# Attention stage of an audio tower: another spacing of the value products, and minima by reductions

## The reference, cut to what matters

```python
hd = C // H; g = hd // 3            # 8 heads of 24 channels, three parts of 8
q3, q4, q5 = (q[..., :g], q[..., g:2 * g], q[..., 2 * g:])   # likewise k and v
x3 = merge(_attn(q4, concat([k3, k4]), concat([v3, v4]), scale))
x4 = merge(_attn(q5, concat([k3, k5]), concat([v3, v5]), scale))
x5 = merge(_attn(q5, concat([k4, k5]), concat([v4, v5]), scale))
out = concat([x3, x4, x5], axis=2);  return out @ w_proj.T + b_proj
```

## Time and profile before

| | |
|---|---|
| median of 3 runs | 1832.63 us (1830.71 to 1834.19) |
| profiled execution | 1832.84 us, span 1831.1 us |
| DVE instructions of attention, first to last block | about 399 to 1381 us of the span |
| busy over the span | PE 95%, DVE 82%, ACT 79%, POOL 68% |
| granted TensorE clock, mean | 0.981 of full speed |

### The profile page before, as it was taken

One profiled execution on the slowest core, in us unless ns is written; L12 is line 12 of the kernel. 1 busy time (PEld: TensorE's weight loads), 2 busy tenths in 40 slices (PEclk: granted clock), 3 DMA queues, 4 the chain that ended last, 5 costly groups with the idle time before them and its releaser, 6 DMA issues. The chain is left out here.

```text
span 1831.1 us, 56113 instructions
## 1 busy us (share of the span) xinstructions
PE 1736.6 (95%) x19008; PEld 1020.6 (56%) x19008; DVE 1497.6 (82%) x3546; ACT 1438.5 (79%) x2983; POOL 1253.9 (68%) x2306
## 2 busy tenths in 40 slices
PE   5999999599999999999999999999984999999999
PEld 3677777244444444444444444444443777777776
DVE  6877777689999999999999999999965555565554
ACT  4667676289999999999999999999974777777775
POOL 5677776467777777777777777777734656565651
PEclk9999999699999999999999999999997999999999
DMA  7344442144444444444444444444431333333232
GB/s 196 93 114 115 115 115 69 28 83 93 92 92 94 93 91 95 92 93 92 92 94 93 90 95 92 93 92 91 94 56 34 73 69 70 70 68 71 65 74 52
DMA packets 503935, 159.49 MB, mean 87 GB/s; under 512 B 452176, under 2 KB 503120, under 8 KB 503888
## 3 DMA queue, kind: packets, MB, share of 16 engines
q1 hardware_dynamic: 503888, 158.90, 41.0%
HBM read 37.26 MB, written 12.48 MB: 27 GB/s over the span
## 5 line engine op out<-in xcount | busy, mean ns | idle before, releaser
L753 DVE TENSOR_REDUCE tops<-p_maxa 128x6 f32<-128x762 f32 x512 | 483.6, 945 | 23.2 <-PE p_maxa L583 22.4
L660 PE MATMUL p_o<-probs,vn 127*32 127x256 f32 x6144 | 411.0, 385 | 0.4 <-DVE att L780 0.4
L703 ACT ACTIVATE probs<-p_s 128x512 f32<-128x512 f32 x512 | 305.3, 596 | 86.1 <-PE p_s L579 85.7
L757 DVE TENSOR_REDUCE tops<-p_maxb 128x4 f32<-128x508 f32 x512 | 346.3, 676 | 0.0
L579 PE MATMUL p_s<-qm,kt 32*128 32x256 f16 x3072 | 341.0, 273 | 3.0 <-DMA qm<-qk 0.7
L710 ACT ACTIVATE probs<-p_s 128x512 f32<-128x512 f32 x512 | 310.7, 607 | 2.3 <-PE p_s L579 2.2
L707 ACT ACTIVATE probs<-p_s 128x512 f32<-128x512 f32 x512 | 304.7, 595 | 0.0
L1062 DVE TENSOR_TENSOR gel_lo<-gel,gel_hi 128x512 f16<-128x512 f32 x192 | 151.7, 790 | 168.6 <-ACT gel_hi L1034 168.5
L579 PEld LDWEIGHTS p_s<-qm,kt 32*128 32x128 f16 x3072 | 135.8, 92 | 223.7 <-issue 127.0
L660 PEld LDWEIGHTS p_o<-probs,vn 127*32 127x32 f32 x6144 | 160.7, 109 | 141.0 <-issue 74.7
L808 POOL TENSOR_TENSOR qk<-raw,one 128x384 f16<-128x384 f32 x128 | 105.9, 827 | 185.4 <-ACT raw L728 185.4
(11 more groups left out here) (212 smaller groups left out, 4529.0 us busy)
## 6 DMA issues: line engine op xcount, KB each, us to landing
xt_a<-in_xt SPq DMA_DIRECT2D x32, 512.0 KB, 4.4
xt_b<-in_xt SPq DMA_DIRECT2D x64, 256.0 KB, 5.2
out<-out_sb SPq DMA_DIRECT2D x32, 336.0 KB, 2.6
xt<-hx SPq DMA_TRANSPOSE x128, 2.4
kt<-qk SPq DMA_TRANSPOSE x128, 2.8
qt<-qk SPq DMA_TRANSPOSE x128, 2.4
qm<-qk SPq DMA_TRANSPOSE x128, 2.7
yt<-ay SPq DMA_TRANSPOSE x128, 2.3
```

The source lines that it names most:

```text
L660: last = nc.tensor.matmul(p_o[32 * j:32 * j + 32, blocks, :], vn[0:NP, r, src:src + 32], probs[0:NP, r % 2, QUAD * g + j, kind * 256:(kind ...
L703: nc.scalar.activation(probs[:, r % 2, h + 1, 0:512], p_s[1][:, :, :].rearrange("p x n -> p (x n)"), ACT.Exp, scale=SCALE).then_inc(act_e1 ...
L753: nc.vector.tensor_reduce(top[:, q, 6 * pair:6 * pair + 6].rearrange("p (e k) -> p e k", e=2), p_ma[:, :, :].rearrange("p (e k) n -> p e k ...
L757: nc.vector.tensor_reduce(top[:, q, 24 + 4 * fourth:28 + 4 * fourth], p_mb[:, :, 0:NP], AX.X, ALU.max, negate=True)\
```

## The change

In PE's order of `attend`, `outputs(., 0, 1)` moves from behind unit 3 of its block to behind unit 0 of the next body, and `outputs(., 1, 0)` from behind unit 0 to behind unit 1. Calls behind units 3, 0, 1 are then one, two, three instead of two, two, two. The minima become three reductions instead of two operations on two tensors; so that each reduces neighbouring elements, the key parts are stored in the order 3, 5, 4 (the weights' columns are permuted on the host, and the names `K3, K5, K4` index them; the `p_maxb` products then read blocks 0 and 2 instead of 0 and 1).

```diff
                 products(i, r, 0)
+                outputs(i - 1, before, 0, 1)
                 outputs(i - 1, before, 0, 2)
+
+                products(i, r, 1)
                 outputs(i - 1, before, 1, 0)
-
-                products(i, r, 1)
                 outputs(i - 1, before, 1, 1)
                 outputs(i - 1, before, 1, 2)
...
                 products(i, r, 3)
                 proj(i)
                 outputs(i, r, 0, 0)
-                outputs(i, r, 0, 1)
...
-                    nc.vector.tensor_tensor(low[:, 0].rearrange("p (g j) -> p g j", g=2), of4[:, 0], of4[:, 1], ALU.min)
-                    nc.vector.tensor_tensor(low[:, 1:3], of5[:, 0:2], of5[:, 2:3].broadcast_to([128, 2, HEADS]), ALU.min).then_inc(dve_min, 1)
+                    nc.vector.tensor_reduce(low[:, 0].rearrange("p (g j) -> p g j", g=2),
+                                            got[:, 24:40].rearrange("p (j g k) -> p g j k", g=2, k=2), AX.X, ALU.min)
+                    of5 = got[:, 0:24].rearrange("p (h k) -> p h k", k=3)
+                    for pair in range(2):
+                        last = nc.vector.tensor_reduce(low[:, 1 + pair], of5[:, :, pair:pair + 2], AX.X, ALU.min)
+                    last.then_inc(dve_min, 1)
...
-                    maximum(p_mb[:, 0:2, :], fourth, 0, slice(0, 2), 0)
-                    maximum(p_mb[:, 2:4, :], fourth, 0, slice(0, 2), 1).then_inc(pe_mb[u], 1)
+                    maximum(p_mb[:, 0:2, :], fourth, 0, slice(K3, K4 + 1, 2), 0)
+                    maximum(p_mb[:, 2:4, :], fourth, 0, slice(K3, K4 + 1, 2), 1).then_inc(pe_mb[u], 1)
```

More of the change, by code:

```diff
@@ L459, in attend @@
         K0 = NQ * 32
+        K3, K5, K4 = range(3)
         scaled, moved = sb("scaled", [128, C]), sb("moved", [128, 1])
@@ L598, in odd @@
                     if do:
-                        score(p_s[1][:, 2:4, :], b, 1, slice(0, 3, 2)).then_inc(pe_s1[u], 1)
+                        score(p_s[1][:, 2:4, :], b, K4, slice(0, 3, 2)).then_inc(pe_s1[u], 1)
                         pe.wait_ge(act_e5[u - 1] if u else act_e5[3], seen(i + 1 if u else i))
-                        score(p_s5[:, 0:2, :], fifth, 2, slice(1, 3), 0)
-                        score(p_s5[:, 2:4, :], fifth, 2, slice(1, 3), 1).then_inc(pe_half[u], 1)
+                        score(p_s5[:, 0:2, :], fifth, K5, slice(1, 3), 0)
+                        score(p_s5[:, 2:4, :], fifth, K5, slice(1, 3), 1).then_inc(pe_half[u], 1)
                 if has_s:
@@ L607, in products @@
                     pe.wait_ge(act_e1[u - 1] if u else act_e1[3], seen(i + 1 if u else i))
-                    score(p_s[1][:, 0:2, :], b, 0, slice(0, 2))
+                    score(p_s[1][:, 0:2, :], b, K3, slice(0, 2))
                 if u == 2:
@@ L616, in products @@
                     pe.wait_ge(act_e0[u - 1] if u else act_e0[3], seen(i + 1 if u else i))
-                    score(p_s[0][:, 0:2, :], a, 0, slice(0, 2))
-                    score(p_s[0][:, 2:4, :], a, 1, slice(0, 3, 2)).then_inc(pe_s0[u], 1)
+                    score(p_s[0][:, 0:2, :], a, K3, slice(0, 2))
+                    score(p_s[0][:, 2:4, :], a, K4, slice(0, 3, 2)).then_inc(pe_s0[u], 1)
                 if has_m:
                     pe.wait_ge(dve_mb[u - 1], seen(i + 2 if u < 3 else i + 3))
-                    maximum(p_mb[:, 0:2, :], fourth, 0, slice(0, 2), 0)
-                    maximum(p_mb[:, 2:4, :], fourth, 0, slice(0, 2), 1).then_inc(pe_mb[u], 1)
+                    maximum(p_mb[:, 0:2, :], fourth, 0, slice(K3, K4 + 1, 2), 0)
+                    maximum(p_mb[:, 2:4, :], fourth, 0, slice(K3, K4 + 1, 2), 1).then_inc(pe_mb[u], 1)
             def rows(o, x, name, bias=None):
@@ L766, in body @@
                     got = top[:, (r + 1) % 2]
-                    of5 = got[:, 0:24].rearrange("p (h k) -> p k h", k=3)
-                    of4 = got[:, 24:40].rearrange("p (j g k) -> p k g j", g=2, k=2)
                     low = slots((r + 1) % 2, 0, NQ)[:, :, 24].rearrange("p (x h) -> p x h", x=3)
-                    nc.vector.tensor_tensor(low[:, 0].rearrange("p (g j) -> p g j", g=2), of4[:, 0], of4[:, 1], ALU.min)
-                    nc.vector.tensor_tensor(low[:, 1:3], of5[:, 0:2], of5[:, 2:3].broadcast_to([128, 2, HEADS]), ALU.min).then_inc(dve_min, 1)
+                    nc.vector.tensor_reduce(low[:, 0].rearrange("p (g j) -> p g j", g=2),
[4 more added lines that the diff above has]
+                    last.then_inc(dve_min, 1)
                 maxima(i, r, 2)
@@ L1193 @@
     v = w[:, 2 * C:].reshape(C, 3, GRP, QUAD, G8).transpose(0, 1, 3, 2, 4).reshape(C, C)
-    arr["wqkv"] = np.concatenate([w[:, C // 3:2 * C], v], axis=1)
+    k3, k4, k5 = (w[:, C + x * C // 3:C + (x + 1) * C // 3] for x in range(3))
+    arr["wqkv"] = np.concatenate([w[:, C // 3:C], k3, k5, k4, v], axis=1)
     arr["wproj"] = np.asarray(L0_attn_w_proj).T.reshape(3, GRP, QUAD, G8, C).transpose(0, 2, 1, 3, 4).reshape(C, C)
```

## The result

The changed kernel takes 1868.45 us (1866.27 to 1870.03, four runs) against 1831.97 of the kernel before beside it: ratio 1.0192, 95% interval 1.0177 to 1.0208. It is slower, by 36 us and not by the 51 of the forecast; that lies at the lower edge of the stated range, just outside it when the ratio is applied to the earlier median (1.0192 x 1832.63 = 1867.8).

A forecast was written before the change was run, and what follows sets the result against it. The prediction took a loop of PE and DVE through unit 2's read as the bound: 0.41 us longer in each of 125 blocks, 51 in all, so 1832.84 + 51 = 1884 us, range 1868 to 1896.

The forecast's parts named there:

- the stated range: Whole kernel: 1868 to 1896 us, meant to hold 8 of 10, around the forecast of 1884.
- What bounds the kernel, and the place of the cost: Loop of PE and DVE through units 0, 1, 2; a third call behind unit 1 makes the block 0.41 us longer.
- first stretch: DVE, from the end of unit 0's p_maxb read to unit 2's p_maxa read: 2.02 us grows to 2.43.
- a second holder of the same place: PE's unit 1: ACT's third exponential, ending at 807.89, also holds it; its getting out of the way buys only 0.02.
- Does the second stretch give it back? ... So no: DVE, unit 2's read to the end of unit 0's next p_maxb read: stays 5.78 us, its idle place unchanged.
- 125 x 0.41 = 51: Sum over attention's 125 steady blocks: each 0.41 us longer, so 51 us more in all.
- Minima: DVE between units 1 and 2: three reductions take 0.3 us instead of 0.52; covered, so they cost or give nothing.
- the 0.4 named: Sign of being right: DVE idle about 0.4 us before line 753 once a block, put down to PE's p_maxa.
- The third: Rival: PE starts unit 1's p_maxb products earlier in some blocks, or DVE's second stretch shrinks; 1858 us, chance 6%.
- The first and second: Rivals: PE's lead holds through units 0 and 1, 1833 us, 3%; DVE's minima set unit 2, 1805 us, 3%.
- The fourth: Rival: ACT's lateness behind the p_o copy adds 0.1 a block, 1897 us, or PE's clock falls, 1891; chance 8%.
- ACT: Copy of p_o starts 0.41 us later; the 0.63 wait at the next unit 0 covers it, with 0.2 left.

The follow-up runs named there:

- e4: Kernel before without POOL's operation that makes the keys' low halves, so that kt and qt are issued earlier: 1825.66 us (0.9955).
- e9: Changed kernel plus one POOL operation (128x192) ahead of the signal that releases the kt and qt DMAs: 1881.11 us (1.0275).
- e3: Changed kernel plus one POOL operation (128x64) ahead of the signal that releases the kt and qt DMAs: 1868.9 us (1.0196).
- e1: Kernel before with only the value products moved as in the changed kernel, minima left as two operations on two tensors: 1867.89 us (1.0189).
- e7: Changed kernel with unit 2's p_maxa products issued before its scores, as in the other units: 1866.55 us (1.0189).

## Why the prediction came out as it did

- *What bounds the kernel, and the place of the cost: right for the changed kernel.* PE's lead won behind unit 3 ended at unit 1's `p_maxb` products, where PE now waits for DVE's read in every block, and the loop through unit 2's read grew from 2.02 to 2.44 in its first stretch, as worked out (2.43). Three calls there take 1.44 (811.73 to 813.17), where two took 1.00. In the kernel before, the profile puts PE's wait in unit 1 down to ACT's third exponential instead (line 710, 29.8 us in 103 blocks), which the forecast had as a second holder of the same place; so the loop named was one of several of nearly the same length, as e4 shows. From the table of waits after:

```profile
PEld p_maxb L584 <- DVE tops L758: 19.3, 99, 0.3
```

- *"Does the second stretch give it back? ... So no": this step failed.* The forecast took the idle time before line 777 as fixed, since the transposes "move with" unit 2's products. They do not keep their distance: in the kernel before, the distance held a wait of PE for the `qt` DMA inside unit 2. With the unit 0.41 later the keys had landed, the unit got 0.13 shorter on average, and DVE's reciprocal stood 1.49 instead of 1.61 behind its read. The term 125 x 0.41 = 51 should have been 125 x (0.41 - 0.13) = 35; measured 36. e9 brings the wait back and pays for it; e4 takes it away in the kernel before, and the wait before the reciprocal goes with it.
- *How it was missed.* The text had the number: `qt` lands at 809.37, "before today's `p_maxa` products of unit 2", so no change. (The trace has 809.41 for this block.) But the unit's scores had started at 809.33, and what should have been compared with the landing was that time, at which the product could have started. That its start followed the landing at the same 0.10 in every block, and not the scores, was the sign of a wait. A steady distance from the issue alone does not show one: before it is 2.52 to 2.56, but the changed kernel keeps 2.68 to 2.71 as closely and does not wait: in e3 the distance is 2.57 and the time is the same. The wait before DVE's read gave no hint, because line 753 hangs on the other of the two products. And the idle time of 0.07 was too small a price for it: the reciprocal also lost the 0.06 by which it could start before the read ahead ends.
- *Minima: right.* Three reductions took 0.33 (812.85 to 813.18; the forecast had 0.3) and changed no time. The idle time before the read is 0.61 rather than the 0.4 named, since it also holds the 0.2 by which the minima got shorter. e1 has the same idle time with two-tensor minima, which no longer started beside line 831.
- *The rivals.* The third, half given back by a shrinking second stretch (1858), named the place but not a mechanism; a third was given back. The first and second did not happen. The fourth had PE's busy share fall to 93.7% and the clock with it; the share is 783.04 of 800, or 97.9%, and the clock stayed at 1.00.
- *ACT.* Its wait before the copy of `p_o` appeared as expected (46.3 us in 99 blocks), and its wait at unit 0 shrank (0.27 in one block, 0.63 before); the time shows no trace of either.

## What to carry to other kernels

A landing ahead of an instruction's start does not mean that nothing waited: compare the landing with the time at which the instruction could have started. Look over many blocks. Here the start kept one distance from the landing (0.10) while its distance from the work ahead varied (0.11 to 0.19), and that was a wait; in a steady loop a constant distance by itself is none. When a change moves work later, list the waits that it lets run out as well as those that it lengthens; part of the price comes back there. Where two engines hold each other at several places of one loop, loosening one place alone can move the idle time to the next, as in e7 and e4.

## What was not expected of the hardware

Products of one unit can start out of their written order, so that "strictly in the written order" above does not hold for the starts on PE. After the change the `p_maxb` product that starts at 813.36 is written behind both `p_maxa` products and starts ahead of the second of them (813.41); so it is in each of 99 blocks, and in none of the 103 before. One `p_maxa` product runs at once with the scores (813.19). The trace does not say which of the two the late one is; by the code it should be the first issued, since that one follows two scores in the same rows of the array. ACT's exponentials of unit 3 take longer in the changed kernel than elsewhere in it:

```profile
808.07 0.67 ACT L708 ACTIVATE probs<-p_s 128x512 f32<-128x512 f32 x1
...
810.00 0.59 ACT L708 ACTIVATE probs<-p_s 128x512 f32<-128x512 f32 x1
```

The first is unit 3's, the second the next unit 0's. The cause was not followed, as ACT waits afterwards.
